# A fused eight-block transformer kernel: the align-attention and ternary feed-forward stage issued in another order

## The reference, cut to what matters

```python
def _L2_xattn_ref(ix, iother, W, b):          # "align"
    ex = ix @ W.T + b
    eother = iother @ W.T + b
    attn = softmax(einsum('bld,bmd->blm', ex, eother))
    return einsum('blm,bmd->bld', attn, iother)

def _ternary_linear(x, w):                    # twice: 256 -> 1024, gelu, 1024 -> 256
    alpha = mean(abs(w))
    w_t = sign(w) * (abs(w) > 0.5 * alpha)
    rms = sqrt(sum(x * x, -1)) / sqrt(d)
    return (x / (rms + 1e-8)) @ w_t.T

x = x + tanh(g_xattn[2]) * _L2_xattn_ref(_layernorm(x), ctx, W, b)
x = x + tanh(g_ffn[2]) * _L2_ffn_ref(_layernorm(x), w_up, w_down)
```

## Time and profile before

| | us |
|---|---|
| median of three runs | 1150.84 (1145.41 to 1151.23) |
| the profiled execution | 1146.76 |
| its span in the profile | 1144.8 |
| align_and_ternary in it | 600.07 to 742.5 |
| first up product | 638.25 |
| PE busy, of the span | 986.6 (86%) |
| DVE busy | 643.0 (56%) |
| ACT busy | 406.3 (35%) |
| POOL busy | 313.9 (27%) |

### The profile page before, as it was taken

How to read it: one execution, slowest core, us unless ns; L and a number is a source line. 1 busy time by engine, 2 the same in 40 slices (tenths; PEclk the granted TensorE clock), 3 DMA queues, 4 the chain that set the end, 5 groups by cost and what they waited for, 6 DMA issues and landing times. The chain is left out here.

```text
span 1144.8 us, 16287 instructions
## 1 busy us (share of the span) xinstructions
PE 986.6 (86%) x5468; PEld 767.4 (67%) x5469; DVE 643.0 (56%) x1281; ACT 406.3 (35%) x650; POOL 313.9 (27%) x287
## 2 busy tenths in 40 slices
PE   4899999979999997767678778779995699999995
PEld 2678878768888885556467567748784466666663
DVE  5768759932122217697775976548686533333331
ACT  2644521211111115686553666265451112121210
POOL 3000001124454431510303445310000244444442
PEclk9999999989999999688896779889998799999998
DMA  4600040026665722020001000017115122222221
GB/s 135 202 1 20 19 130 25 32 74 188 188 191 171 218 36 73 1 74 1 0 2 37 1 1 1 0 42 283 38 38 177 48 46 46 46 46 46 45 42 19
DMA packets 67810, 79.61 MB, mean 70 GB/s; under 512 B 12656, under 2 KB 52171, under 8 KB 67755
## 3 DMA queue, kind: packets, MB, share of 16 engines
q1 hardware_dynamic: 54123, 60.27, 16.0%
q0 software_dynamic: 13632, 18.62, 9.5%
HBM read 60.73 MB, written 17.83 MB: 69 GB/s over the span
## 5 line engine op out<-in xcount | busy, mean ns | idle before, releaser
L2607 PE MATMUL ps<-w_L_ffn_w,room 128*128 x312 | 149.0, 601 | 0.6 <-DVE room L2769 0.6
L269 POOL TENSOR_TENSOR norm_vec<-norm_vec,powers 128x4 f32<-128x4 f32 (+3 forms) x27 | 29.6, 1097 | 373.4 <-DVE norm_vec L263 372.5
L2571 POOL DMA_INDIRECT out_x<-f_yo,f_give x39 | 61.9, 1588 | 122.8 <-DVE f_yo L2786 119.7
L2404 DVE TENSOR_TENSOR room<-room,ps 128x1024 f32<-128x1024 f32 x24 | 29.3, 1220 | 110.9 <-issue 81.6
L2673 ACT ACTIVATE room<-ps 128x512 f32<-128x512 f32 x39 | 23.3, 597 | 181.4 <-PE ps L2607 181.4
L2607 PEld LDWEIGHTS ps<-w_L_ffn_w,room 128*128 128x128 f32 x312 | 57.0, 193 | 42.3 <-issue 40.4
L2205 PE MATMUL ps<-b_room,room 128*128 128x256 f32 x384 | 85.0, 379 | 0.0
L2171 POOL DMA_INDIRECT acc_rows<-f_eo,f_idx x32 | 52.4, 1637 | 100.4 <-DVE f_eo L2433 51.6
L2205 PEld LDWEIGHTS ps<-b_room,room 128*128 128x128 f32 x384 | 72.9, 190 | 9.9
L430 PE MATMUL ps<-a_vblk,a_pT 128*128 128x51 f32 (+1 forms) x640 | 74.7, 272 | 0.0
L2622 PE MATMUL ps<-w_L_ffn_w,room 128*128 x312 | 73.9, 380 | 0.9 <-DVE room L2774 0.9
(11 more groups left out here) (373 smaller groups left out, 2125.3 us busy)
## 6 DMA issues: line engine op xcount, KB each, us to landing
w_L_ffn_w<-in_L_ffn_w SPq DMA_DIRECT2D x24, 512.0 KB, 8.8
b_room<-in_L_ffn_Wg SPq DMA_DIRECT2D x16, 512.0 KB
b_room<-in_L_ffn_Wu SPq DMA_DIRECT2D x16, 512.0 KB
b_room<-in_L_ffn_Wd SPq DMA_DIRECT2D x16, 512.0 KB, 6.7
xn_rows<-xn_sb SPq DMA_DIRECT2D x8, 512.0 KB, 2.9
x_sb<-in_x SPq DMA_DIRECT2D x4, 512.0 KB, 6.8
xn_sb<-in_L_ffn_w SPq DMA_DIRECT2D x2, 1024.0 KB, 7.8
x_sb<-acc_rows SPq DMA_DIRECT2D x4, 512.0 KB, 5.6
```

The costliest lines, as they stand in the source:

```text
L269: pool.tensor_tensor(nv[:, 7, lo:hi], nv[:, 6, lo:hi], self.K.npow[:, lo:hi], ALU.pow).then_inc(self.s_pow, 1)
L2571: pool.indirect_dma_start(out_rows[:, :], bass.IndirectOffsetOnAxis(ap=give[:, j:j + 1], axis=0), yo[j % 2][:, :], None, compute_op=ALU.ad ...
L2607: m = pe.matmul(ps[:, banks[p], :], xsT[p][:, i * P:(i + 1) * P], w[:, e, i, :], start=(i == 0), stop=(i == KT - 1))
```

## The change

Five edits, all in one go.

1. The first transposes, their copies and the scores of group 0 move into the one-bit stage's last tiles (`first_turns`, `first_copies`, `first_scores`); the transposed rows are kept over the border of the two stages.
2. In align_and_ternary every engine's list is written in another order: group 0's attention and its feed-forward preparation come first, the attention of groups 2 and 3 is spread between up(0, f) and up(1, f), and the row preparation of groups 2 and 3 into the loop. ACT begins with two one-element activations that load its tables, Exp first, Gelu later.
3. The signs of the down weights are made in four pieces of 512 columns between other work; the loads that overwrite those weights wait for the last piece (s_set 20 in place of 14).
4. From tile 4 on down uses four banks, and in the last group two down products stand ahead of squares.
5. In top2_ffn lo, the lane table and in_lane are all 16-bit, the table has the tile index innermost, POOL makes it ahead (a copy of 128 x 2048 at the start of multihead), and DVE needs two instructions in place of four.

```diff
+    def first_turns(self, pe):
+        for u in range(2):
+            pe.wait_ge(self.by_pool, 2 * u + 2)
+            ... 4 transposes into bank 2 + u ...
+    def first_copies(self, act): ... two copies to K.xnT ...
+    def first_scores(self, pe):
+        pe.wait_ge(self.s_copied, 2)
+        self.scores(pe, 0, 0)
...
+        SCORES = (0, 1, 3, 3)
+        def out_bank(n):
+            return 4 + n % 4 if n >= 4 else 4 + n % 2
...
-                sp.wait_ge(tw.s_set, 14)
+                sp.wait_ge(tw.s_set, 20)
...
-                    if n >= 2:
+                    if n < 2:
+                        pe.wait_ge(a_x, 7 + n)
+                    elif n < 6:
                         pe.wait_ge(x_done, n - 1)
+                    elif n < 8:
+                        pe.wait_ge(x_lo, n + 1)
                     else:
-                        pe.wait_ge(a_x, 7 + n)
+                        pe.wait_ge(x_done, n - 3)
...
 PE:   turn_a(2) turn_p(0) values(0) turn_a(3) scores(1) turn_a(4) turn_x(0) turn_p(1) turn_x(1) values(1)
       up(0,0) turn_a(5) up(0,1) scores(2) up(0,2) turn_a(6) up(0,3) turn_a(7) up(0,4) scores(3) up(0,5)
       turn_x(2) turn_x(3) up(0,6) turn_p(2) up(0,7) values(2); in the loop turn_p(3) after up(1,0),
       values(3) after up(1,1), turn_x(2g+2), turn_x(2g+3) after up(g,4); at the end
       down(3,0) down(3,1) squares(3) down(3,2) down(3,3)
 ACT:  table exps(0) copy_a(2) copy_p(0) copy_a(3) rows 8-11 rows_x(0) copy_a(4) exps(1) copy_p(1) table
       high_part(0,1) hidden(0,0) copy_a(5) hidden(0,1) hidden(0,2) copy_a(6,7) rows_x(1) hidden(0,3)
       hidden(0,4) exps(2) exps(3) hidden(0,5) high_part(2,3) copy_p(2) hidden(0,6) hidden(0,7) copy_p(3)
 DVE:  front(0) moments of tiles 8-15 weigh(0) signs(0) attended(0) moments(0) signs(1) scale_rows(0)
       front(1) weigh(1) low_part(0,1) attended(1) moments(1) split(0,0) signs(2) scale_rows(1) split(0,1)
       front(2) split(0,2) signs(3) split(0,3) front(3) split(0,4) low_part(2,3) split(0,5) weigh(2,3)
       split(0,6) attended(2,0) split(0,7) attended(2,1) split(1,0) moments(2) attended(3,0) split(1,1)
       scale_rows(2) attended(3,1), then the loop
 POOL: root, rows 12 13, spreads(0), rows 14 15, add_square(0,1), add_square(0,2), spreads(1), ...
...
-                    for t in (0, 8):
-                        dve.tensor_tensor(in_lane[:, n, t:t + 8, :], lo[:, n, t:t + 8].unsqueeze(2).broadcast_to([P, 8, P]),
-                                          ahead.lane[:, :].unsqueeze(1).broadcast_to([P, 8, P]),
-                                          ALU.is_equal).then_inc(cells, 1)
+                    dve.tensor_tensor(in_lane[:, n, :, :], lo[:, n, :].unsqueeze(1).broadcast_to([P, P, NT]),
+                                      ahead.lanes[:, :, :], ALU.is_equal).then_inc(cells, 1)
```

More of the change, by code:

```diff
@@ L1021, in _ @@
                         if g == 1 and f == 0:
-                            turn_x(6)
-                            turn_x(7)
+                            turn_p(3)
+                        if g == 1 and f == 1:
+                            values(3)
                         if f == 3:
@@ L1027, in _ @@
                             down(g - 1, DOWN.index(f))
+                        if g < 3 and f == 4:
+                            turn_x(2 * g + 2)
+                            turn_x(2 * g + 3)
+                down(NG - 1, 0)
+                down(NG - 1, 1)
                 squares(NG - 1)
-                for i in range(4):
-                    down(NG - 1, i)
+                down(NG - 1, 2)
+                down(NG - 1, 3)
             @block.scalar
@@ L1274, in residual @@
                     dve.bn_stats(K.st[:, n, :], xt)
+                front(0)
                 dve.wait_ge(side.stat, NT)
                 side.norm.moments(dve, 1)
-                tw.signs(dve, 1, td, h[:, :, :].rearrange("p a w -> p (a w)"), slice(0, FT * D))
+                weigh(0)
+                down_signs(0)
+                attended(0, 0)
                 side.norm.shift(dve, 1)
-                front(0)
+                attended(0, 1)
+                moments(0)
+                down_signs(1)
@@ L1281, in _ @@
+                scale_rows(0)
                 front(1)
[L1282 to L1285 removed]
                 weigh(1)
[L1287 to L1292 removed]
                 low_part(0)
                 low_part(1)
[L1295 to L1296 removed]
+                attended(1, 0)
@@ L1297, in _ @@
+                attended(1, 1)
+                moments(1)
                 split(0, 0)
-                weigh(3)
+                down_signs(2)
+                scale_rows(1)
                 split(0, 1)
-                scale_rows(2)
+                front(2)
+                split(0, 2)
+                down_signs(3)
+                split(0, 3)
+                front(3)
+                split(0, 4)
                 low_part(2)
                 low_part(3)
-                split(0, 2)
-                attended(3)
@@ L1305, in _ @@
-                moments(3)
-                split(0, 3)
-                split(0, 4)
-                scale_rows(3)
                 split(0, 5)
-                low_part(4)
-                low_part(5)
+                weigh(2)
+                weigh(3)
                 split(0, 6)
+                attended(2, 0)
                 split(0, 7)
+                attended(2, 1)
+                split(1, 0)
+                moments(2)
+                attended(3, 0)
+                split(1, 1)
+                scale_rows(2)
@@ L1314, in _ @@
+                attended(3, 1)
                 for g in range(1, NG):
                     for f in range(FT):
-                        split(g, f)
-                        if g == 1 and f == 0:
-                            low_part(6)
-                            low_part(7)
+                        if g > 1 or f > 1:
+                            split(g, f)
+                        if g == 1 and f == 2:
+                            moments(3)
+                        if g == 2 and f == 1:
+                            scale_rows(3)
+                        if g < 3 and f == 4:
+                            low_part(2 * g + 2)
+                            low_part(2 * g + 3)
```

267 lines of the change are left out of this document (143 added, 124 removed).

## The result

The changed kernel takes 1143.43 us in the median of its 20 runs (1138.03 to 1151.40); 20 runs of the kernel before on the same chips have a median of 1150.03. The ratio is 0.9953 (95% interval 0.9932 to 0.9974). By this ratio it is 5.4 us faster, and just inside what I called no change (0.5%); the forecast was 17.5 us, and the time lies above the range.

What follows compares the result with a forecast made beforehand. No engine bound the block throughout; it lost time in the front, DVE-paced groups 0 and 1, and PE's waits before down(g, 2). Terms -13.7 + 6.0 - 8.9 - 0.4 - 0.5 = -17.5 us; forecast 1131 us, range 1118 to 1142.

Steps and rivals of the forecast that it cites:

- Front: Block's start up to the first up product: -13.7 us, first up at 624.5 in place of 638.25, bounds 621 and 628.
- Groups 0 and 1: Block's stretch after the first up, with moved-in work behind it: +6.0 us, 54.5 against 48.5, bounds 48.5 and 62.
- Groups 2 and 3: Loop's later turns: four banks end PE's waits for residuals, PE sets the pace at 17.9 and 16.1 us; -8.9 us.
- The tail: Block's end after down(2,3): 10.6 us in place of 11.0, PE's last downs hidden behind DVE; -0.4 us.
- top2_ffn: Routing's in_lane: gain 1.0 us as middle of bounds, less 0.5 for strided weight loads; -0.5 us.
- Multihead: Stage behind the block: POOL's table copy stands ahead of roots not due for tens of us; nothing to 1 us.
- C: Rival: DVE is slowed beside POOL's sums of squares in groups 0 and 1; some 1140 us, chance 0.12.
- D: Rival: four banks do nothing, another wait replaces the residual's at down(g, 2), groups 2 and 3 unchanged; 1140 us, chance 0.07.

## Why the forecast was wrong, step by step

- **Front, -14.5 as a length.** Measured -15.2; up(0,0) came at 621.84 against a forecast of 624.5 with bounds of 621 and 628. Right, also in PE's level: the mean clock is 0.51 to 0.61 there in the three profiles, mostly the lower level that the list assumed. The scores in the one-bit stage's tail cost 0.7 us, from PE's last product of that stage to the block's start (595.98 to 599.49, against 597.26 to 600.07), and the forecast had 0.8.
- **Groups 0 and 1, +6.0.** This step failed: +11.9 (58.0 to 61.5 us for the stretch, just inside the upper bound of 62, against 54.5). The forecast let DVE set the pace: 49.7 us of its work, and 4.8 of waiting. Its own list did not add up to that, for it named waits of 5 to 9 us for POOL and of 3 for ACT, 8 to 12 on DVE alone. DVE's work came to 43.8 to 47.6 us, less than forecast: the 40.3 us that I started from held splits lengthened by POOL's sums (16 in 15.2 us), and in the new order the 16 took 11.0 to 13.0. DVE's idle time came to 13.7 to 17.6 us in place of 4.8. The named waits were near their sizes, one below and one above: 6.0 and twice 4.1 us for POOL (5 to 9), 2.98 for ACT, 4.1 to 5.1 on PE before down(0,2) (forecast 2.6), and 3.4 to 4.3 more on DVE for a GELU at the end, as before. What the sum had no term for is PE. It got 48 more instructions, 8.5 us, and it pays for a wait twice, in the wait and in products at the lower level behind it: taking the one wait before down(0,2) away gave 8.4 us in the stretch. The wait that I ranked first (POOL's power) was worth 0 to 3, since ACT's list and the same residual stood behind it.
- **Groups 2 and 3, -8.9.** Measured -7.0. The four banks did it: in this order they are worth 11 us by the timed runs, and 12 in the two stretches. The two kept 2.4 and 1.4 us more than the forecast's 17.9 and 16.1, less the 1.9 that I had kept back. Two edits take that away, and they overlap: with POOL's power early they are 16.8 and 16.9, with the sums short 18.0 and 16.1.
- **The tail, -0.4.** Failed: +3.2. My list began the tail with free splits. In DVE's list split(3,7) stands behind factors(2), whose two tensor_scalar steps took 1.2 us each beside sums, and behind two residuals. PE waits 3.24 us, and the late squares then leave four residuals to run one behind the other. From there to the end it is 10.4 us, so the forecast's 10.6 held and the 3.24 us of waiting were the term it lacked. Another order of the list took 2.7 us of the tail away in the profile.
- **top2_ffn, -0.5.** Measured -2.3, and 1.7 over all twenty profiles. in_lane ran at double rate, a gain of 2.2 us, as the rule of the Trainium skill (VectorE: DVE Perf Modes, What auto-detection actually checks) had it; I had taken the middle of my bounds instead. The weight loads took 1.5 to 1.6 times as long; what that cost was not measured apart.
- **Multihead, 0 to +1.** +3.6 in the mean of three profiles, by the clock alone: PE's idle time there is the same to 0.4 us. Of the kernels with the old block, three profiles have 144.2 or 144.3 us there and a fourth, in an execution whose front was 6 us longer too, 145.9; those with the new block have 144.2 to 150.5 in sixteen, and only one of them is as short as the three. That speaks for the new order making the late return of the clock likelier, but no run shows how.
- **Rivals.** C (DVE beside POOL, 1140 us) comes nearest in time, and the sums are costly as it said in kind. But it had them enter the stretch with the change, and they were there before: POOL is busy 24.0 us in groups 0 and 1 before and 23.4 after, and shortening the sums took as much from the block in the kernel before. So it does not explain the difference, and that its number is near is luck. D (four banks do nothing) is refuted.

The misses sum up: +5.9 in groups 0 and 1, +3.6 in the tail, +3.6 in multihead, +1.9 in groups 2 and 3, less 0.7 in the front and 1.8 at the routing: 12.5 us, which is what lies between the forecast's lengths (-18.3 without the later start) and the measured -5.8.

## What to carry to other kernels

A wait of PE in a stretch where it was running cost here about twice its length, once as a gap and once at the lower clock (4.1 to 5.1 us of wait, 8.4 us of the stretch); look at the products behind each gap, and price a gap by both. A forecast by the engine that sets the pace needs a second sum for the others, with the work that moves in: here PE's 8.5 us were in none. A wait that a profile shows at the head of a chain need not be worth its length: take it away and see what stands behind it, and take the ones further down first (here the output banks of the first group, 7 us in the block, before POOL's power, 0 to 3). When short steps of one engine have two durations (0.17 and 1.2 us over 4 columns), look at once for what the neighbour ran at that moment: shortening the sums took more from the block (16 us) than the reordering did (7), and the cost was there before the change. The best kernels here combine the edits and reach 0.978 to 0.980 of the time before, 1126 to 1127 us.

## What the runs showed of the hardware

- A DVE step with both inputs in SBUF, or a cast or tensor_scalar from SBUF, that starts while POOL runs a sum of 128x512 is held until that sum is over: a step over 4 columns ends 0.02 to 0.03 us behind it (0.17 us becomes 1.24), a cast of 512 columns 0.28, a split of 512 columns 0.55. Steps that read PSUM and at most one SBUF tile, the reciprocal and bn_stats are not held (0.48, 0.18 and 0.43 us inside a sum).
- The block has 28 such sums of 1.25 to 1.82 us. With sums over 8 columns it is 16 us shorter in either order, by held steps and by POOL being done sooner together.
- A 16-bit step of 128x2048 with one operand repeated along its middle dimension ran in 1.218 us, the time of 1024 columns of the earlier form.
- Weight loads of 128x128 in 16 bit with a step of 16 elements take 154 and 163 ns, against 98 and 111 to 112 without.
- PE's clock was back at the upper level some 10 or 18 us after the start of one and the same wait of 4.00 us, in executions of programs with the same PE work in that stage; such differences move a stage of 144 us by up to 6 us. The block's start, behind an identical program, moved by 8 us.
